# A decoder layer with routed experts: the experts are turned and split in the first iteration and kept in memory as halves

## The reference

```
x = x + self_attention(norm(x))          # 16 heads of 32, rotary factors, causal, Wq Wk Wv Wo with biases
x = x + cross_attention(norm(x), ctx)    # 16 heads; ctx is 16 x 722 x 384, keys and values from kv_w
x = x + experts(norm(x))                 # below
gates = softmax(x @ gate_w.T + gate_b)               # 8 experts
top_gates, top_idx = top_k(gates, 2)
out = sum over the two of top_gates * (x @ expert_w[e].T + expert_b[e])
```

## Time and profile before

| | before |
|---|---|
| median of three runs | 1280.93 us |
| the profiled execution | 1280.48 us |
| its span | 1278.7 us |
| mean granted TensorE clock | 0.975 |
| busy: PE, DVE, ACT, POOL | 93%, 65%, 50%, 57% |
| memory read and written | 60.13 and 30.36 MB |

### The profile page before, as it was taken

How to read it: one execution, slowest core, us unless ns; L and a number is a source line. 1 busy time by engine, 2 the same in 40 slices (tenths; PEclk the granted TensorE clock), 3 DMA queues, 4 the chain that set the end, 5 groups by cost and what they waited for, 6 DMA issues and landing times.

```text
span 1278.7 us, 43327 instructions
## 1 busy us (share of the span) xinstructions
PE 1194.4 (93%) x19120; PEld 806.8 (63%) x19120; DVE 830.7 (65%) x1455; ACT 642.2 (50%) x946; POOL 729.6 (57%) x690
## 2 busy tenths in 40 slices
PE   4789899999999999999999999999999877699997
PEld 4456576767667676767676767676767555555543
DVE  4658476858585867676767777677777586423156
ACT  4335556556565656565656464646565535533300
POOL 1436656667676766667675857575757455500042
PEclk9799999999999999999999999999999988799999
DMA  8010611010202010101011110101010345455356
GB/s 302 2 42 2 240 44 50 3 59 3 66 4 65 17 44 9 53 17 52 19 50 32 38 48 12 43 17 52 17 58 11 116 159 190 146 159 170 131 163 212
DMA packets 47840, 93.28 MB, mean 73 GB/s; under 512 B 3775, under 2 KB 15351, under 8 KB 47655
## 3 DMA queue, kind: packets, MB, share of 16 engines
q1 hardware_dynamic: 44135, 79.03, 18.7%
q0 software_dynamic: 3520, 11.47, 2.9%
HBM read 60.13 MB, written 30.36 MB: 71 GB/s over the span
## 4 chain that ended last, share of the span: by engine, by line
PE 86%; DVE 4%; DMA 3%; POOL 3%; ACT 2%; issue 1%; another core or an unknown queue 1%; SPq 1%; ACTq 0%; DVEq 0%
PE psum L323 56%; PE psum L922 7%; PE psum L1025 6%; PE psum L1010 5%; PE psum L940 2%; PE psum L899 2%; PE psum L891 1%; DMA bank<-in_L_attn_Wv 1%; DMA out<-bank 1%; PE psum L967 1%; PE psum L855 1%; PE psum L907 1%; DVE xT L1176 1%; POOL bank L1444 1%
## 5 line engine op out<-in xcount | busy, mean ns | idle before, releaser
L1444 POOL TENSOR_TENSOR bank<-prob,bank 128x1200 f16<-128x1200 f32 x128 | 314.6, 2468 | 188.4 <-ACT bank L1120 188.3
L1268 DVE TENSOR_REDUCE c_most<-psum 100x4 f32<-100x1444 f32 x128 | 211.6, 1653 | 14.7 <-PE psum L1010 12.6
L323 PE MATMUL psum<-bank,cT 128*128 128x512 f16 (+1 forms) x864 | 198.7, 379 | 0.1
L323 PE MATMUL psum<-cT,bank 128*128 128x361 f16 x1152 | 196.1, 321 | 0.0
L1111 ACT ACTIVATE prob<-psum 128x1200 f32<-128x1200 f32 x128 | 150.0, 1172 | 76.6 <-PE psum L1025 62.4
L1176 DVE TENSOR_TENSOR cv<-psum,cv 128x512 f16<-128x512 f32 x125 | 86.0, 688 | 107.4 <-ACT cv L1102 57.2
L1120 ACT ACTIVATE bank<-prob 128x1200 f16<-128x1200 f32 x128 | 151.7, 1198 | 1.4
L323 PEld LDWEIGHTS psum<-cT,bank 128*128 128x128 f16 x1152 | 106.1, 99 | 65.5 <-DVE c_raw L1195 3.0
L323 PEld LDWEIGHTS psum<-bank,cT 128*128 128x128 f16 (+1 forms) x864 | 85.1, 101 | 88.2 <-issue 4.1
L1102 ACT ACTIVATE cv<-psum 128x512 f16<-128x512 f32 x96 | 57.4, 598 | 149.9 <-PE psum L323 148.3
L1229 DVE SCALAR_TENSOR_TENSOR bank<-psum,b_part,bank 128x361 f16<-128x361 f32 x128 | 74.4, 592 | 81.1 <-ACT bank L1088 81.1
(11 more groups left out here) (215 smaller groups left out, 1905.8 us busy)
## 6 DMA issues: line engine op xcount, KB each, us to landing
c_raw<-in_ctx SPq DMA_DIRECT2D x16, 960.0 KB
xs_scratch<-y_kept SPq DMA_DIRECT2D x1, 7424.0 KB, 22.8
c_raw<-xs_scratch SPq DMA_DIRECT2D x29, 256.0 KB, 2.7
ys_scratch<-bank SPq DMA_DIRECT2D x29, 256.0 KB, 2.0
bank<-in_L_ffn_expert_w SPq DMA_DIRECT2D x7, 1024.0 KB, 7.7
x_in<-in_x SPq DMA_DIRECT2D x16, 200.0 KB
x_scratch<-x_out SPq DMA_DIRECT2D x16, 200.0 KB
y_kept<-x_scratch SPq DMA_DIRECT2D x10, 256.0 KB, 3.2
```

Of the source, the lines that this page charges most:

```text
L323: last = pe.matmul(out_ap, a(pa), b(pb), start=(i == 0 and j == 0), stop=(i == len(pairs) - 1 and j == 2))
L1268: dve.tensor_reduce(c_most[:, hf], score[0:L, :, 0:HC], AXIS.X, ALU.max).then_inc(max_done, 1)
L1444: pool.tensor_tensor(prob16[o % 2][:, (2 + part) * PT:(3 + part) * PT], prob[:, part], prob16[o % 2][:, part * PT:(part + 1) * PT], ALU.su ...
```

## The change

The turning moves to iteration -1. Two raw buffers (`raw_e`: the probabilities' float32 buffer, and space of the second key buffer) are filled in turn by `load_raw`; FW writes into two buffers in the space of the split probabilities (`w_made`), and `store_made` puts each finished expert, both halves, 1 MB, into a new tensor `wT_dram` in memory. A raw buffer is loaded again when the expert two before it is done, and the store stands ahead of that load in SyncE's order. `load_expert` now loads the finished halves straight into slot e: experts 0 to 2 after SV of iteration 14, 3 after OP, 4 to 7 at the start of iteration 15. FW stands two per step in steps 2 to 17 of iteration -1. In iteration 14 the gate and route steps come one step earlier (FS10 and FN10 both in step 9), as do TT and TP; SC1 moves from iteration 15 to 14, and later scatters come earlier in iteration 15. The padding of the keys is zeroed at the end of iteration -1, because a raw buffer lies over it.

```diff
-GATE_EXTRA = {10: ["FS10"], 11: ["FN10"], 12: ["FX10"], 13: ["FL10"], 14: ["RT00", "RE0"], 15: ["RT01"], 16: ["RT02"],
-              17: ["RT03", "RP"], 18: ["FR"], 19: ["SC0"]}
+GATE_EXTRA = {9: ["FS10", "FN10"], 11: ["FX10"], 12: ["FL10"], 13: ["RT00", "RE0"], 14: ["RT01"], 15: ["RT02"],
+              16: ["RT03", "RP"], 17: ["FR"], 18: ["SC0"], 19: ["SC1"]}
+FIRST_EXTRA = {2: ["FG0"], 7: ["BV0", "BV1"]}
+for e in range(E):
+    for k in range(KD):
+        FIRST_EXTRA.setdefault(2 * e + 2 + k // 2, []).append(f"FW{e}{k}")
 LAST_STEPS = [
-    ["low3a", "A0", "max_A0", "SC1", "FW00", "FW01"],
-    ["B0", "max_B0", "low3b", "FW02", "FW03"],
-    ["MX0", "SC2", "FW10"],
-    ["T0a", "exp0a", "PV3", "FW11", "PL"],
...
+    ["low3a", "A0", "max_A0"],
+    ["B0", "max_B0", "low3b"],
+    ["MX0", "SC2"],
+    ["T0a", "exp0a", "PV3", "SC3", "PL"],
+    ["T0b", "exp0b", "high0a", "scale_heads"],
+    ["A1", "max_A1", "low0a", "high0b"],
+    ["B1", "max_B1", "low0b", "TT"],
+    ["MX1", "SC4"],
+    ["T1a", "exp1a", "SC5", "TP"],
+    ["T1b", "exp1b", "high1a", "PV0"],
...
+    ["MX2", "SC6", "FS11"],
+    ["T2a", "exp2a", "FN11", "SC7"],
...
+    ["MX3", "SC8"],
+    ["T3a", "exp3a", "SC9"],
+    ["T3b", "exp3b", "high3a", "PV2", "high3b", "SC10"],
@@ steps_of
-    every = [list(step) for step in (moved(STEPS, "TP", 7) if n == B - 2 else STEPS)]
+    every = [list(step) for step in (moved(moved(STEPS, "TT", 5), "TP", 6) if n == B - 2 else STEPS)]
@@ build_layer
+        def load_raw(sp, e):
+            if e >= 2:
+                sp.wait_ge(chunk_out, its[-1].done(f"FW{e - 2}{KD - 1}"))
+            sp.dma_start(raw_e[e % 2], eW[e].rearrange("(o p) h -> p o h", p=P)).then_inc(raw_e_loaded[e % 2], 16)
+
+        def store_made(sp, e):
+            sp.wait_ge(chunk_out, its[-1].done(f"FW{e}{KD - 1}"))
+            sp.dma_start(wT_dram[e], prob16[e % 2][:, 0:KD * 2 * D]).then_inc(w_stored[e % 2], 16)
+
         def load_expert(sp, e):
-            sp.dma_start(raw_e[e], eW[e].rearrange("(o p) h -> p o h", p=P)).then_inc(e_loaded[e], 16)
+            if e == 0:
+                for i in range(2):
+                    sp.wait_ge(w_stored[i], 16 * E // 2)
+            sp.dma_start(bank[:, e * KD * 2 * D:(e + 1) * KD * 2 * D], wT_dram[e]).then_inc(e_loaded[e], 16)
@@ sync_iteration
                 sp.wait_ge(chunk_out, it.done("SV"))
-                for e in range(2):
+                for e in range(3):
                     load_expert(sp, e)
...
+            if n < 0:
+                for e in range(6):
+                    store_made(sp, e)
+                    load_raw(sp, e + 2)
             if n < B - 2:
                 sp.wait_ge(chunk_out, it.done("SO"))
                 load_ctx(sp, n + 2)
...
@@ end_loads
             all_scattered(sp)
-            sp.wait_ge(chunk_out, its[B - 1].done("FW73"))
+            sp.wait_ge(chunk_out, its[B - 2].done("SO"))
@@ act_chunk, FW
+                e = int(name[2])
+                if e == 1:
+                    act.wait_ge(w_low, 2)
+                elif e >= 2:
+                    act.wait_ge(w_stored[e % 2], 16 * (e // 2))
+                op = act.activation(w_made[e % 2][:, int(name[3]), 0], f[:, 0:D], ACT.Copy, scale=WSCALE)
```

More of the change, by code:

```diff
@@ L116, in moved @@
     return [[c for c in step if c != name] + ([name] if h == to else []) for h, step in enumerate(steps)]
-GATE_EXTRA = {10: ["FS10"], 11: ["FN10"], 12: ["FX10"], 13: ["FL10"], 14: ["RT00", "RE0"], 15: ["RT01"], 16: ["RT02"],
-              17: ["RT03", "RP"], 18: ["FR"], 19: ["SC0"]}
-LAST_STEPS = [
-    ["low3a", "A0", "max_A0", "SC1", "FW00", "FW01"],
-    ["B0", "max_B0", "low3b", "FW02", "FW03"],
-    ["MX0", "SC2", "FW10"],
-    ["T0a", "exp0a", "PV3", "FW11", "PL"],
[L126 to L141, removed]
@@ new lines @@
+GATE_EXTRA = {9: ["FS10", "FN10"], 11: ["FX10"], 12: ["FL10"], 13: ["RT00", "RE0"], 14: ["RT01"], 15: ["RT02"],
[4 more added lines that the diff above has]
+        FIRST_EXTRA.setdefault(2 * e + 2 + k // 2, []).append(f"FW{e}{k}")
+LAST_STEPS = [
+    ["low3a", "A0", "max_A0"],
[8 more added lines that the diff above has]
+    ["T1b", "exp1b", "high1a", "PV0"],
+    ["A2", "max_A2", "low1a", "high1b"],
+    ["B2", "max_B2", "low1b"],
+    ["MX2", "SC6", "FS11"],
+    ["T2a", "exp2a", "FN11", "SC7"],
+    ["T2b", "exp2b", "high2a", "PV1"],
+    ["A3", "max_A3", "low2a", "high2b", "FX11"],
+    ["B3", "max_B3", "low2b", "FL11"],
+    ["MX3", "SC8"],
+    ["T3a", "exp3a", "SC9"],
+    ["T3b", "exp3b", "high3a", "PV2", "high3b", "SC10"],
@@ L341, in build_layer @@
         y_again = [y_kept[:, (t + 3) % 4] for t in range(EARLY)]
-        raw_e = [(bank[:, (e + 1) * KD * 2 * D:(e + 2) * KD * 2 * D].bitcast(F32) if e < E - 1 else
-                  c_flat[:, 0:KD * D]).rearrange("p (o h) -> p o h", o=KD) for e in range(E)]
+        raw_e = [r.rearrange("p (o h) -> p o h", o=KD)
+                 for r in (prob[:].rearrange("p i n -> p (i n)")[:, 0:KD * D], flat32[:, 2 * KD * D:3 * KD * D])]
+        w_made = [prob16[i][:, 0:KD * 2 * D].rearrange("p (k s f) -> p k s f", k=KD, s=2) for i in range(2)]
+        wT_dram = nc.dram_tensor("wT_scratch", (E, P, KD * 2 * D), F16, kind="Internal").ap()
         xn_dram = nc.dram_tensor("xn_scratch", (EARLY * P, D), F32, kind="Internal").ap()
@@ L385, in build_layer @@
         e_loaded = [sem(f"e_loaded{e}") for e in range(E)]
+        raw_e_loaded = [sem(f"raw_e_loaded{i}") for i in range(2)]
+        w_stored = [sem(f"w_stored{i}") for i in range(2)]
         f_bn, f_stats, f_half, f_rstd, f_norm = (sem(n) for n in ("f_bn", "f_stats", "f_half", "f_rstd", "f_norm"))
@@ L532, in pe_slots @@
                 pe.wait_ge(experts_ready, 1)
+                for e in range(E):
+                    pe.wait_ge(e_loaded[e], 16)
             pe.wait_ge(chunk_out, its[B].done(f"ST{j}"))
@@ L770, in sync_iteration @@
                 load_x(sp, n + 2)
+            if n < 0:
+                for e in range(6, E):
+                    store_made(sp, e)
             if n == B - 2:
@@ L786, in last_loads @@
             sp.wait_ge(exp_done, 2 * GROUPS * (B - 1))
-            for e in range(3, E - 1):
+            for e in range(4, E):
                 load_expert(sp, e)
             for t in range(4, EARLY):
-                if t == 8:
+                if t == 9:
                     sp.wait_ge(chunk_out, it.done("TP"))
@@ L838, in _ @@
             sp.dma_start(raw_p, cWp.rearrange("(k p) f -> p k f", p=P)).then_inc(p_loaded, 16)
+            sp.wait_ge(bias_done, 1)
+            sp.wait_ge(wT_low, 4 * KD)
+            for e in range(2):
+                load_raw(sp, e)
             sp.wait_ge(w_low, 3)
@@ L955, in pe_chunk @@
                 e, k = int(name[2]), int(name[3])
-                pe.wait_ge(e_loaded[e], 16)
+                pe.wait_ge(raw_e_loaded[e % 2], 16 * (e // 2 + 1))
                 for o in range(KD):
-                    last = pe.transpose(f[:, o * P:(o + 1) * P], raw_e[e][:, o, k * P:(k + 1) * P], ident[:])
+                    last = pe.transpose(f[:, o * P:(o + 1) * P], raw_e[e % 2][:, o, k * P:(k + 1) * P], ident[:])
             elif kind == "FX":
@@ L1115, in act_probs_high @@
             g = GROUPS * it.n + o
+            if g < 2:
+                act.wait_ge(w_stored[g], 16 * E // 2)
             if part == 0 and g >= 2:
@@ L1307, in dve_iteration @@
                             dve.memset(prob16[i][:, 4 * PT:], 0.0).then_inc(prob_padded, 1)
+                if n < 0 and h == len(it.steps) - 1:
+                    dve.memset(split_k_all[:, :, :, :, LC:].rearrange("p i s k c -> p (i s k) c"), 0.0)\
+                       .then_inc(k_padded, 1)
                 for name in step:
```

12 lines of the change are left out of this document (3 added, 9 removed).

## The result

The changed kernel takes 1297.89 us, median of four runs, against 1280.99 for the kernel before on the same chip: ratio 1.0131, 95% interval 1.0113 to 1.0148. It is slower, as forecast, but by 16.9 us where 6 were forecast. The profiled execution took 1296.02 us (span 1294.3, 1278.7 before; mean granted clock 0.963 after 0.975).

The account below looks back on a forecast made before the run. TensorE was taken as the bound except in iteration -1 and from iteration 14's end through 15, where it waits on other engines. 1280.48 + 15.4 + 4.5 - 13.5 = 1286.9, said as 1287 us; range 1273 to 1297.

Parts of the forecast that it names:

- Iteration -1: Cost of turning the experts there: 15.4 us, first cross scores of iteration 0 at 110.3; ends 6.1 and 22.9.
- first scores: Iteration -1, first self-attention scores on TensorE: +2.45 us, from 46.75 to 49.2, behind the later CX5.
- from CV2 to A0: Last part of iteration -1: 5.4 us for 14 transpose groups less a wait, plus 0.75 for the padding memset.
- The stalls under full memory queues: Rival, iteration -1: three TensorE stalls, 7.5 us, as memory sets the pace; 1294.4 us in all, chance 0.12.
- Iterations 0 to 14: Cost of a new wait in iteration 14: +4.5 us, ends -2 and +6.5.
- The wait at FS10: Iteration 14, statistics of token tile 10: VectorE stands 6 us, its tile loaded after x2's store, behind three experts.
- Iteration 15: Gain from taking out the experts' turning: slots start 17.1 or 10.9 us earlier, 13.5 taken; ends 7 and 17.5.
- GpSimd's sum: Iteration 15: 50.0 us of operations and scatter gaps without waits; with about 3.5 us of waits, last scatter near 1095.
- that of the cross scores: Iteration 15: 10.3 us per head group, four groups and projection 44 us at full clock, about 58 at half.
- iteration 15 above 62 us: Sign of being wrong: first cross scores to slots' loads still above 62 us, where 52 to 58 were forecast.
- almost without gaps: Sign of being right: GpSimd working in iteration 15 with almost no gaps.
- iteration 15 is not relieved: Rival: GpSimd and the unseen waits hold iteration 15, gain only 7 us; 1293.4 us in all, chance 0.13.

Follow-up runs that it names:

- the repaired kernel: Changed kernel with the store of x2 first and iteration 15's scatters one at a time, each behind a TensorE report: 1290.49 us, ratio 1.0064.

## Why the prediction was wrong

The sign and the place of each cost were right; the gain of iteration 15 was put at twice its size, and the time came out 0.9 us above the range.

Iteration -1: 15.4 us forecast, 17.1 measured. The start was put too high (first scores +1.1, not +2.45; CV2 +7.7, not +9.3) and the last part too low: from CV2 to A0 it is 9.4 us more, not 6.15. The two misses partly cancel, so the total is nearer than its terms. Between CV2 and A0 TensorE waited 1.75 us for raw expert 6, which I had not counted, and before CV2 2.33 us for expert 4 instead of 1.25; the run without reloads gives 3.0 us for both. The 1.7 us by which the total is off is no more than profiles differ by: A0 comes at 94.9 to 97.3 us in the four profiles that turn in iteration 15, and at 111.3 to 113.8 in the nine that turn here with reloads, 16.4 us later on average. The stalls under full memory queues that made a rival did not come.

Iterations 0 to 14: 4.5 forecast, 5.1 measured. The wait at FS10 is 5.2 us (some 6 forecast), its cause the store behind three experts, as the run with the store first shows; the 2.81 us of FX10 went.

Iteration 15 is the step that failed: 13.5 us forecast, 7.2 measured; its 6.3 us are most of the error of 9.1 (1296.0 against 1286.9). The prediction saw 10.9 us of waits without a source on the chain of before, but left only "about 3.5 us of waits" in GpSimd's sum and none in that of the cross scores. Measured, GpSimd's waits in iteration 15 were 14.3 us (10.7 before the lows, 3.6 before the scaling), and the exponentials' unseen waits 19.9. The prediction thus let such waits shrink, though nothing in the profile said that they belonged to the work taken out. One of its own signs of being wrong came: iteration 15 above 62 us (62.1 to the slots' load), with GpSimd busy 40.38 of them and not "almost without gaps". The unseen waits belong to the scatters, which the change keeps: what the scatters hold costs 9.4 us of d before and 11.2 after. Without them the estimate was good: the slots' load would come 55.1 us after A0, within the 52.2 to 58.4 of the prediction (1097.3 and 1103.5, less 1045.1). The rival "iteration 15 is not relieved" had the size right, 7 us, and half of the reason: the unseen waits held, GpSimd's own work did not (d 52.6 with GpSimd fully busy).

The other half of the answer is the turning itself. It stood on 16.4 us of the chain but is worth 5 to 7, with the late reports or without: where it goes, the scores' own sequence of maximum, turning and exponential is late next, 13.2 to 14.5 us a group even without scatters (its exponentials start at 1077.0, 1090.3, 1104.8 and 1118.0 with plain stores). In iteration -1, where TensorE was busy 43.34 of 48.2 us, the same 32 groups cost their full time. That is most of the loss: work moved from where TensorE waits anyway to where it doesn't. The wait for token tile 10 is most of the rest.

The clock from A0 to the slots' load was 0.60, and holding it at 0.89 gave 2.6 us of d. The Trainium skill, "TensorE: Matmul & The Clock Gate", HAM oscillation, let one expect the slow clock here, and the trace agrees.

What stays open: why an indirect transfer's issue on GpSimd delays TensorE's reports, and in places its products. Shown is that neither GpSimd's arithmetic, nor the traffic of the rows, nor plain stores issued by GpSimd do it. And the repaired kernel keeps 2.8 us of d (56.1 with single scatters, 53.3 with plain stores). Its trace still has four reports of TensorE late by 0.7 to 1.7 us, each 0.4 to 0.7 us after a scatter; how much of the 2.8 us they make is not shown.

## What to carry to other kernels

A share of the chain is not the gain of taking work out: ask what is late next, and cost moved work by the idle time at either place. Waits without a source must be tied to a cause before they are let shrink; look what runs on every engine when they end. Put indirect transfers where no report of TensorE is awaited; one at a time they still hold reports, and that placement alone gained only 2 to 3 us of time here.

## What had not been expected of the hardware

While GpSimd issues indirect stores of 128 rows (0.98 us each), TensorE's report of finished products can arrive 1.3 to 5.6 us late in the changed kernel, 0.5 to 1.1 us after the run of stores ends. A report early in a run can be on time or late. MX in the changed kernel was on time, with the first scatter from 1119.59, products' end at 1120.56 and record at 1120.57. T2b was 2.06 us late, with the first scatter from 1109.27, products' end at 1110.13 and record at 1112.20. Single stores between reports cost less (d 56.1 against 64.9), but not nothing. ScalarE's and VectorE's records inside the run of MX (1120.95 and 1121.31) were on time. Three operations of 128 x 512 float32 in a row on GpSimd took 1.49 us each against 0.77 for the norm's single one in the same trace; the cause was not looked for.
